# Two of four column chunks of the turned rows loaded in the last two steps of the first stage

## What is computed

```python
x = x + tanh(g_xattn[0]) * xattn0(layernorm(x), ctx, ctx, Wq, bq, ... Wo, bo)
x = x + tanh(g_ffn[0])   * ffn0(layernorm(x), controller, f1, f2, bias)
x = x + tanh(g_xattn[1]) * xattn1(layernorm(x), ctx, ctx, mask)
x = x + tanh(g_ffn[1])   * ffn1(layernorm(x), ln_g, ln_b, w1, w2)
```

```python
logits = einsum('...btd,des->...btes', grouped, controller) + tie
perm   = (logits == max(logits, axis=-3, keepdims=True))
sel    = einsum('...btd,...btes->...besd', grouped, perm)      # the gather
inner  = relu(einsum('...besd,desf->...besf', sel, f1) + bias)
inter  = einsum('...besf,esfd->...besd', inner, f2)
```

## Time and profile before

| | |
|---|---|
| time, median of 3 executions | 1412.21 us (1411.93 to 1413.98) |
| time of the profiled execution | 1412.67 us |
| its span, first to last instruction | 1410.6 us |
| mean granted clock of TensorE | 0.915 of full speed |
| busy: PE, DVE, ACT, POOL | 1185.2, 948.2, 687.5, 521.4 us |
| phase 1 ends, the gather stage begins (first transfer issued) | 566.2 us |
| first gather matmul | 571.3 us |
| gather stage: last copy of an output | 818.1 us |

### The profile page before, as it was taken

How to read it: one execution, slowest core, us unless ns; L and a number is a source line. 1 busy time by engine, 2 the same in 40 slices (tenths; PEclk the granted TensorE clock), 3 DMA queues, 4 the chain that set the end, 5 groups by cost and what they waited for, 6 DMA issues and landing times. The chain is left out here.

```text
span 1410.6 us, 25197 instructions
## 1 busy us (share of the span) xinstructions
PE 1185.2 (84%) x9040; PEld 877.5 (62%) x9040; DVE 948.2 (67%) x2229; ACT 687.5 (49%) x1130; POOL 521.4 (37%) x448
## 2 busy tenths in 40 slices
PE   5899999999999985599999829999921189944998
PEld 5788888888888873476666405556611178842443
DVE  5567677776766763245453326999957699886875
ACT  3334444343443432123434415666636389747993
POOL 1233333333333423078676613666640000002452
PEclk9999999999999996699999969999965589976999
DMA  6223322222323311967878889999423079843994
GB/s 221 76 91 103 118 97 90 90 90 98 104 98 104 105 54 60 338 232 289 284 279 297 309 304 387 331 332 332 159 65 90 1 175 373 338 194 126 418 375 155
DMA packets 127907, 274.35 MB, mean 194 GB/s; under 512 B 44320, under 2 KB 55616, under 8 KB 121152
## 3 DMA queue, kind: packets, MB, share of 16 engines
q1 hardware_dynamic: 114144, 235.21, 46.4%
q0 software_dynamic: 10688, 36.71, 7.7%
q10 hardware_dynamic: 2976, 1.14, 0.3%
HBM read 155.32 MB, written 109.31 MB: 188 GB/s over the span
## 5 line engine op out<-in xcount | busy, mean ns | idle before, releaser
L2307 POOL DMA_DIRECT2D p_y<-residual x32 | 27.6, 866 | 275.4 <-POOLq L113 244.2
L1842 PE MATMUL p_z<-qT,w1T 128*128 128x256 bf16 (+1 forms) x1152 | 114.3, 263 | 11.9 <-DMA qT<-p_q 11.9
L966 PEld LDWEIGHTS p_sel<-p_pick,p_xp 128*128 128x128 bf16 x1536 | 91.7, 102 | 49.6 <-issue 36.1
L1842 PEld LDWEIGHTS p_z<-qT,w1T 128*128 128x128 bf16 x1152 | 102.6, 99 | 23.4 <-DMA qT<-p_q 11.9
L966 PE MATMUL p_sel<-p_pick,p_xp 128*128 128x128 bf16 x1536 | 103.2, 227 | 16.0 <-DMA p_xp<-xparts 9.8
L1113 DVE COPY p_selT<-p_sel 128x512 f32<-128x512 f32 x64 | 44.3, 692 | 103.8 <-PE p_sel L966 103.8
L2328 PE MATMUL p_o<-w2T,p_Gq 128*128 128x512 bf16 x384 | 86.5, 386 | 6.0 <-DVE p_Gq L2375 6.0
L1057 ACT ACTIVATE p_selT<-p_sel 128x512 f32<-128x512 f32 x64 | 38.2, 597 | 84.5 <-PE p_sel L966 84.5
L614 POOL TENSOR_TENSOR p_rs<-p_ve,p_mhalf 128x2 f32<-128x2 f32 x32 | 22.3, 698 | 151.7 <-DVE p_ve L680 151.6
L357 PE MATMUL p_M<-p_ctxTh,p_Wkh 128*128 128x256 f32 x256 | 75.7, 296 | 1.9 <-DVE p_Wkl L690 1.9
L357 PE MATMUL p_M<-p_xnTh,p_Wqh 128*128 128x256 f32 x256 | 75.0, 293 | 1.1 <-DVE p_V L763 1.1
(11 more groups left out here) (329 smaller groups left out, 3502.4 us busy)
## 6 DMA issues: line engine op xcount, KB each, us to landing
inter_d<-p_stage SPq DMA_DIRECT2D x64, 512.0 KB, 4.3
p_rows<-inter_d SPq DMA_DIRECT2D x32, 1024.0 KB, 8.9
activations<-hid SPq DMA_DIRECT2D x20, 1024.0 KB, 7.1
p_cin<-in_ctx_dram SPq DMA_DIRECT2D x32, 512.0 KB, 5.5
xparts<-p_parts SPq DMA_DIRECT2D x16, 768.0 KB, 3.2
activations<-third SPq DMA_DIRECT2D x12, 1024.0 KB, 7.2
hid<-activations SPq DMA_DIRECT2D x12, 1024.0 KB, 15.5
p_xp<-xparts SPq DMA_DIRECT2D x3, 3072.0 KB, 24.9
```

Of the source, the lines that this page charges most:

```text
L966: mm = pe.matmul(bsel[u % 2][:, k * P:(k + 1) * P], xp[:, c, tile, r, :], pick[sb % 2][:, tile, :, :].rearrange("p s g -> p (s g)"), start ...
L1842: mm = pe.matmul(bank, w1T[:, c, fc * P:(fc + 1) * P], qT[:, bass.ds(first, tiles), c, :], start=(c == 0), stop=(c == C - 1))
L2307: pool.dma_start(y[n % YR][:, :], x3_d[:, token_tile(n), :]).then_inc(s[f"x_in{n % YR}"], 16)
```

## The change

Three pairs of weight tiles (k, v, q, high and low) are no longer tiles of `phase1`: they become views of two larger tiles `early[0]` and `early[1]`, 128 partitions x 24 KB each, that live through both stages. When Wk, Wv and Wq have been used for the last time, SP loads batches 0 to 13 (`EARLY` = 14 of 16) of the column chunks 0 and 1 from `xparts` into them, in step 16, behind the store of the last residual, 2688 KB each. In the gather stage SP then loads the last two batches of chunks 0 and 1 (384 KB each) and chunks 2 and 3 whole. Chunk 0 is loaded there in one piece, and gather(0) waits for it before its last unit (u = 7), not in parts.

```diff
+EARLY = B - 2
+
+def early_parts(early, c):
+    return early[c][:, :, :].bitcast(BF16).rearrange("p a n -> p (a n)").rearrange("p (t r k) -> p t r k", t=TILES, r=3)
...
-        W = {w: (sbt(f"W{w}h", [P, C, D], F32R), sbt(f"W{w}l", [P, C, D], F32R)) for w in "qkvo"}
+        rooms = [room[:, k, :].rearrange("p (c n) -> p c n", c=C) for room in early for k in range(3)]
+        W = {w: (rooms[2 * i], rooms[2 * i + 1]) for i, w in enumerate("kvq")}
+        W["o"] = sbt("Woh", [P, C, D], F32R), sbt("Wol", [P, C, D], F32R)
...
                     sp.dma_start(x_mid[b - 1], x1[1 - par][:, :, :]).then_inc(s["x1_out"], 16)
+                if M and not F:
+                    sp.wait_ge(s["kT_done"], 2 * B)
+                    sp.wait_ge(s["qT_done"], 2 * B)
+                    sp.wait_ge(s["parts_out"], 16 * EARLY)
+                    for c in range(len(early)):
+                        sp.dma_start(early_parts(early, c)[:, 0:EARLY * NT, :, :].rearrange("p (b t) r k -> p b (t r k)", t=NT),
+                                     xparts[0:EARLY, :, c, :, :, :].rearrange("b p t r k -> p b (t r k)")).then_inc(s["early_in"], 16)
...
             sp.wait_ge(s["gmask_in"], 16)
+            sp.wait_ge(s["early_in"], 16 * len(early))
...
-        xp = sbt("xp", [P, C, TILES, 3, P], BF16)
+        NEARLY = len(early)
+        later = sbt("xp", [P, C - NEARLY, TILES, 3, P], BF16)
+        xp = [early_parts(early, c) for c in range(NEARLY)] + [later[:, c, :, :, :] for c in range(C - NEARLY)]
...
             def load_xp(c):
-                sp.dma_start(xp[:, c, :, :, :].rearrange("p (b t) r k -> p b (t r k)", t=NT),
-                             xparts[:, :, c, :, :, :].rearrange("b p t r k -> p b (t r k)")).then_inc(s[f"xp_in{c}"], 16)
-
-            for k in range(C):
-                q = B // C
-                sp.dma_start(xp[:, 0, k * NT * q:(k + 1) * NT * q, :, :].rearrange("p (b t) r k -> p b (t r k)", t=NT),
-                             xparts[k * q:(k + 1) * q, :, 0, :, :, :].rearrange("b p t r k -> p b (t r k)")).then_inc(s[f"xp_in0_{k}"], 16)
+                first = EARLY if c < NEARLY else 0
+                sp.dma_start(xp[c][:, first * NT:TILES, :, :].rearrange("p (b t) r k -> p b (t r k)", t=NT),
+                             xparts[first:B, :, c, :, :, :].rearrange("b p t r k -> p b (t r k)")).then_inc(s[f"xp_in{c}"], 16)
+
+            load_xp(0)
...
                     if q == 0 and u % 2 == 0:
                         pe.wait_ge(s["pick_done"], u // 2 + 1)
-                        pe.wait_ge(s[f"xp_in0_{u // 2}"], 16)
+                    if q == 0 and u == EARLY * NT // BANK:
+                        pe.wait_ge(s["xp_in0"], 16)
...
+        with ExitStack() as e1:
+            early = [e1.enter_context(nc.sbuf_tensor(f"early{c}", [P, 3, C * D], F32R)) for c in range(2)]
+            phase1(..., early)
+            phase2a(..., early)
```

More of the change, by code:

```diff
@@ L156, in shape_constants, with phase1 @@
     }
-def phase1(nc, x, ctx, gx, Wq, bq, Wk, bk, Wv, bv, Wo, bo, ctrl, K, x_mid, xparts, perm, groupmask, vg_d, w1, w2, asum):
+EARLY = B - 2
+def early_parts(early, c):
+    return early[c][:, :, :].bitcast(BF16).rearrange("p a n -> p (a n)").rearrange("p (t r k) -> p t r k", t=TILES, r=3)
+def phase1(nc, x, ctx, gx, Wq, bq, Wk, bk, Wv, bv, Wo, bo, ctrl, K, x_mid, xparts, perm, groupmask, vg_d, w1, w2, asum, early):
     xt = x.rearrange("b (t p) d -> b p t d", p=P)
@@ L244, in phase1 @@
             logits_full logits_taken pmT_done aside_sp aside_pe aside_dve
-            in_k in_v in_q in_o w_high w_low ident_in const_in tanh_done tgbo_done abs_in0 abs_in1 abs_done0 abs_done1""".split()
+            early_in in_k in_v in_q in_o w_high w_low ident_in const_in tanh_done tgbo_done abs_in0 abs_in1 abs_done0 abs_done1""".split()
         s = es.enter_context(semaphores(nc, "p1_", names))
@@ L825, with phase2a @@
 BANK = 4
-def phase2a(nc, xparts, perm, gmask, f1, bias, f2, K, inter_d, w1, w2, asum, gam, th, nth, tern_d):
+def phase2a(nc, xparts, perm, gmask, f1, bias, f2, K, inter_d, w1, w2, asum, gam, th, nth, tern_d, early):
     RING, WN = 4, 2
@@ L852, in phase2a @@
         names = """bias_in f1_in0 f1_in1 f2_in0 f2_in1 pick_done sel_full sel_act sel_dve f1_used inner_full inner_done
-            bias_full bias_done lay_full lay_act lay_dve w_in0 w_in1 w_step tern_out consts sums_full tsum_done gamma_done th_done""".split() + [f"xp_in{c}" for c in range(1, C)] + [f"xp_in0_{k}" for k in range(C)] + \
+            bias_full bias_done lay_full lay_act lay_dve w_in0 w_in1 w_step tern_out consts sums_full tsum_done gamma_done th_done""".split() + [f"xp_in{c}" for c in range(C)] + \
             [f"stage_out{i}" for i in range(RING)]
@@ L965, in gather @@
                         for r in range(3):
-                            mm = pe.matmul(bsel[u % 2][:, k * P:(k + 1) * P], xp[:, c, tile, r, :],
+                            mm = pe.matmul(bsel[u % 2][:, k * P:(k + 1) * P], xp[c][:, tile, r, :],
                                            pick[sb % 2][:, tile, :, :].rearrange("p s g -> p (s g)"), start=(r == 0), stop=(r == 2))
@@ L2435, in mk_flamingo_gated @@
         perm, gmask = sbt("perm", [P, TILES, SL], BF16), sbt("groupmask", [P, GR])
-        phase1(nc, x, ctx, gx, Wq, bq, Wk, bk, Wv, bv, Wo, bo, ctrl, K, x_one, xparts, perm, gmask, vg_d, w1, w2, asum)
         gam, th, nth = [sbt(n, [P, 2]) for n in ("gam", "th", "nth")]
-        phase2a(nc, xparts, perm, gmask, f1, bias, f2, K, inter_d, w1, w2, asum, gam, th, nth, tern_d)
+        with ExitStack() as e1:
+            early = [e1.enter_context(nc.sbuf_tensor(f"early{c}", [P, 3, C * D], F32R)) for c in range(2)]
+            phase1(nc, x, ctx, gx, Wq, bq, Wk, bk, Wv, bv, Wo, bo, ctrl, K, x_one, xparts, perm, gmask, vg_d, w1, w2, asum, early)
+            phase2a(nc, xparts, perm, gmask, f1, bias, f2, K, inter_d, w1, w2, asum, gam, th, nth, tern_d, early)
         cand = sbt("cand1", [P, NC1])
```

## The result

The changed kernel takes 1400.61 us (median of 5 runs, 1396.7 to 1403.9) against 1412.21 before (5 runs, 1411.88 to 1413.98): a ratio of 0.9913, 95% interval 0.9902 to 0.9924, so 11.6 us less. The forecast was 1397.8 in a range of 1394.8 to 1402.0: right in direction and inside the range, the gain (14.4) 2.8 us too large. The profiled execution took 1401.04 us, 11.6 less than that of before, so the traces can be compared row by row.

A forecast was written before the change was run, and what follows sets the result against it. The prediction took the gather stage to be bound by loads up to 600 us, then by PE. hidden(0) 14.7 us earlier, less 0.3 for near ties, gave a gain of 14.4: 1412.21 to 1397.8 us, range 1394.8 to 1402.0.

The forecast's parts named there:

- its own case: The forecast as worked out, 1397.8 us, with its own range of 1396 to 1400 us; chance 0.66.
- the transfers set more of it: Rival: larger slip (5.5 us) and chunk 2 landing 2 us later; gain 11.2, time 1401 us; chance 0.14.
- signs of being wrong: Late SP issue at 561.25, slower step 17, gather(2) waiting over 1 us, or clock rising over 5.3 us after gather's start.
- The bound of the stage: Gather stage: up to 600 us it goes at the pace of the loads, from there at PE's.
- The loads into rooms in step 16: Early loads of 5.505 MB, issued at 548.7 and 549.1, flow from 551.0 until 565.8 at 373 GB/s.
- gather(0) and gather(1) in one run: Start of the gather stage: both gathers without holes take 14.7 us, so hidden(0) starts 14.7 us earlier.
- The slip: End of phase 1: the last xparts store stands behind the early loads, ending 3.8 us later (bounds 2.6 and 5.5).
- The wait for chunk 2: Before gather(2): chunk 2 lands at 589.5, needed at 589.76, so it fits by 0.3 us.
- near tie: Chunks 2 and 3 land just before they are needed; 0.3 us charged for the two.
- Chunk 3: Before gather(3): chunk 3 lands at 599.3, needed at 599.8.
- The faster loads: Rival: early loads run at 404 GB/s, slip 2.6, gain 15.9, time 1396.3 us; chance 0.10.
- The slower rival: Early loads move far slower, at 233 GB/s giving 1406.6 us; a loss under 188 GB/s; chance 0.04.

The follow-up runs named there:

- e0_again: The changed kernel again with no edit: 1401.58 us, ratio 0.9925 to the kernel before.
- e3_loads_twice: Changed kernel, but the gather stage loads all four chunks again, so the early loads are of no use: 1417.86 us, ratio 1.0033 to the kernel before.
- e5_small_on_act: Changed kernel with early loads in step 15 and the gather stage's two small loads (ident, bias_r) issued by ACT: 1396.42 us.
- e6_in_parts: Changed kernel with early loads in step 15, chunks 2 and 3 loaded in four parts each and PE waiting by parts: 1395.54 us.
- e7_store_act: Changed kernel with the last store of xparts issued on ACT's queue instead of SP's: 1399.92 us.
- e1_step15: Changed kernel with the early loads issued in step 15 instead of step 16: 1396.87 us, ratio 0.9888 to the kernel before.
- e2_one_chunk: Changed kernel with only chunk 0 loaded early, chunk 1 loaded whole in the gather stage: 1406.19 us, ratio 0.9951 to the kernel before.

## Why the prediction was right, and where it was too high

The time came out inside the range, but just outside the 1396 to 1400 us that the prediction gave its own case at 0.66: 1400.61 lies in the stretch of the rival "the transfers set more of it", which had 0.14. Of the signs of being wrong that it names, one came true, a wait of over 1 us for chunk 2. The others did not: SP issued the last store as soon as POOL had its parts ready, step 17 took its 12.9 us from residual to last store as before, and the clock was back 3 us after the gather's start.

**The bound of the stage** was read rightly: the loads up to 600 us, PE from there, and everything behind moved as a block. The 12.06 us won at gather(2) were 11.9 at the next stage and 11.6 at the end.

**The loads into rooms in step 16** went as worked out. Both were issued by 551.64, not by 549.6 (the issuing took 2.12 us for two, not 0.43 each), which cost nothing, as the next wait ended at 561. The DMA engines were full from 552 to 568, over most of the loads at the rate that was taken:

```profile
560.00:561.00 1.00, 0.00 (x0) 0.00 (x0) 0.00 (x0) 0.00 (x0) 1.00 (x1) 0.50 1.06 372
```

**gather(0) and gather(1) in one run**: 14.7 us forecast, 14.73 measured, and 14.72 to 15.35 over the five other profiles with both in one run. The hit to 0.03 us is in part luck: 1.4 of the 14.7 us were a choice between two costs of the clock. The delay from the stage's first issue to the first gather matmul, 1.49 forecast, was 1.44.

**The slip** is the first term that was mis-sized: 3.8 forecast, 4.57 measured (4.42 to 4.57 in the four profiles with loads of this size in step 16), within its bounds of 2.6 and 5.5. I let the last bytes end at 567.8, and at 568.5 if phase 1's 0.7 us are added; nearly all of them did. But the engines do not end together. The windows of a quarter of a us, changed kernel:

```profile
568.25:568.50 0.25, 0.00 (x0) 0.00 (x0) 0.00 (x0) 0.00 (x0) 0.00 (x0) 0.50 0.60 246
568.50:568.75 0.25, 0.00 (x0) 0.00 (x0) 0.00 (x0) 0.00 (x0) 0.00 (x0) 0.50 0.08 25
568.75:569.00 0.25, 0.00 (x0) 0.00 (x0) 0.00 (x0) 0.00 (x0) 0.00 (x0) 0.50 0.06 25
569.00:569.25 0.25, 0.00 (x0) 0.00 (x0) 0.00 (x0) 0.00 (x0) 0.00 (x0) 0.50 0.06 25
```

A busy share of 0.06 is one engine of sixteen: it was still at work 0.7 us after the others, and the wait for the store ended only after it was through. Before, no such tail followed the store alone:

```profile
563.75:564.00 0.25, 0.00 (x0) 0.00 (x0) 0.00 (x0) 0.00 (x0) 0.00 (x0) 0.50 0.55 221
564.00:564.25 0.25, 0.00 (x0) 0.00 (x0) 0.00 (x0) 0.00 (x0) 0.00 (x0) 0.50 0.01 0
```

In this profile that tail is the missing 0.8 us. The other profiles with loads of this size have nearly the same slip with another tail. In e0_again one engine is alone for about 0.5 us; in e3_loads_twice the busy share is still 0.49 in 568.75 to 569.00 and 0.12 in the quarter behind it, then 0: more engines go on longer and stop closer together. What the four have in common is the last byte, 7.1 to 7.3 us after the store's issue, where the sum had 567.8 - 561.25 = 6.55. Why it comes later than bytes and rate give is not shown; no run was made on it.

**The wait for chunk 2**, for which 0.3 us were charged, took 1.08 (1.50 in the second profile). The near tie was seen, and the term that was mis-sized in it is the landing: 19.5 us after the stage's first issue in the sum, 20.9 measured (573.33 + 19.0 - 571.46). I scaled it by 352 GB/s, from a stage in which large transfers followed each other without a gap. Two things differ. In the new order four small transfers stand first, and in the first 4.5 us after the first issue 0.70 MB moved, against 0.94 in the kernel before and 1.01 in e5_small_on_act; at 373 GB/s the 0.24 MB are 0.6 us. And 352 is not the rate of the engines but only of the bytes that I counted: until the awaited chunk had landed SP's queue had moved 7.14 MB in the kernel before, where I counted 6.37, and 4.97 in the changed kernel, where I counted 4.01. The uncounted part, which grew by 0.2 MB or 0.5 us, can only belong to loads behind the awaited one. The two make 1.1 of the 1.4 us. e5_small_on_act and e6_in_parts each removed the wait.

With chunk 2 late, the two gathers no longer decide when gather(2) starts. It starts when chunk 2 is there, 20.7 to 21.3 us after the first issue in the changed kernel, e0_again and e7_store_act, also in e7_store_act, whose two gathers take 0.6 us longer.

**Chunk 3** was in time as forecast: gather(3) follows hidden(1) without a hole.

Sum at gather(2): 14.8 (14.73 in place of 29.54), less 1.6 (the later start, of which 0.7 is phase 1's clock in this execution), less 1.1 (chunk 2) = 12.1. Of the 2.3 us between this and the forecast's 14.4, 0.8 are the slip, 0.8 chunk 2, 0.7 the clock. The rival "the transfers set more of it" (gain 11.2) was thus nearer in time than the forecast, with smaller amounts in both its places: 4.6 and 1.1 instead of 5.5 and what 2 us more at chunk 2 give. The faster loads did not come: 369 to 378 GB/s over most of the early loads, so the time worked out from the 436 GB/s of the Trainium skill ("DMA: Bandwidth & Descriptors", "Anatomy of one DMA — SWDGE (gpsimd) path"), 1395.1, was too good here; the trace doesn't agree with that price for these loads. The section gives it for transfers that GpSimd issues, and SP issued these. (The 17.1 us of gain worked out with it still hold the 0.3 us for near ties that it says fall away; without them it is 17.4.) The slower rival was excluded by the same rows.

**What the change left.** Its step is late by one. Everything that the early loads wait for (the last use of Wq at 516, the store of batch 13 landed by 521) is true in step 15, where the DMA engines have little to do (a busy share of 0.08 in 523 to 540 before); in step 16 the loads end behind the store that ends the phase. e1_step15 wins 4.7 us more for one edited line.

## What to carry to other kernels

A load that is moved into an earlier stage isn't free because the engines wait for nothing there: ask which transfer ends that stage, and whether the moved bytes are through before it is issued. Here 5.5 MB in the last 13 us gave back 4.6 of some 16 us, and the same bytes 27 us sooner gave back none. Another queue for the store didn't help, nor did fewer bytes, since the rest only came due in the next stage. Where a large transfer is awaited to within a us, look at what is issued ahead of it, or let its reader wait for it in parts; either took away the wait, but what it was worth was too little to be told by the time.

## What the runs showed of the hardware that was not expected

After 5.5 MB of loads in pieces of 1536 bytes and a store behind them, one of the 16 DMA engines was 0.7 us behind the others in the changed kernel's profile and about 0.5 in e0_again's; behind a store alone they ended within 0.2 us. In e3_loads_twice the engines ended nearly together, at the same distance from the store's issue. The landing worked out from bytes and rate was 0.6 to 0.75 us too early in the four profiles with such loads in step 16.

Issuing two loads of 1792 pieces took SP 2.12 us, of which the first takes 0.39 (e2_one_chunk, with one load, took 0.39); the second was held 1.7 us though it fitted, by count, in what the queue had held before. In the gather stage of before, three loads of 2048 pieces went out in 0.43, 13.3 and 7.9 us; what decides how long the second is held was not tested.
